# Attention scores of each head in four column tiles of 32 keys, with the queries of a chunk read from one of two fixed buffers

## What is computed

```python
B, N, C = x.shape                      # 4, 4096, 128
q, k, v = jnp.split(jnp.einsum('bnc,ce->bne', x, W_qkv), 3, axis=-1)
...                                    # each to (B, N, 4 heads, 32)
q = l2norm_axis1(q)
k = l2norm_axis1(k)
sim = jnp.einsum('bihd,bjhd->bhij', q, k) * SCALE
attn = jax.nn.softmax(sim, axis=-1)
out = jnp.einsum('bhij,bjhd->bhid', attn, v)
...
return jnp.einsum('bne,ec->bnc', out, W_out) + b_out
```

## Time and profile before

| | |
|---|---|
| median of 3 runs | 6119.24 us (6114.16 to 6120.37) |
| the profiled execution's own time | 6126.93 us |
| its span, first to last instruction | 6125.1 us |
| mean granted TensorE clock | 0.943 of full |
| attention, each of 4 images | about 571 us |
| from one chunk's reciprocal to the next | 70.51 us in most chunks |
| PE / DVE / ACT busy in those 571 us | 552.28 / 518.54 / 495.73 us |

### The profile page before, as it was taken

How to read it: one execution, slowest core, us unless ns; L and a number is a source line. 1 busy time by engine, 2 the same in 40 slices (tenths; PEclk the granted TensorE clock), 3 DMA queues, 4 the chain that set the end, 5 groups by cost and what they waited for, 6 DMA issues and landing times. The chain is left out here.

```text
span 6125.1 us, 76011 instructions
## 1 busy us (share of the span) xinstructions
PE 4839.5 (79%) x21528; PEld 1764.6 (29%) x21592; DVE 5167.2 (84%) x5922; ACT 3730.4 (61%) x4769; POOL 2009.7 (33%) x1562
## 2 busy tenths in 40 slices
PE   5777779996676778999667667899966667789996
PEld 2222422222322242222232224222233222422223
DVE  6799679998679967999868996799976899689987
ACT  1666378882266637888126663788812666378881
POOL 2488500003148850000414884000041588400004
PEclk8899989999889999999888999899988899999998
DMA  1000020000000002000000000200000000020000
GB/s 37 0 1 0 14 53 0 0 0 14 28 0 1 0 14 53 0 0 0 14 28 0 1 0 14 53 0 0 0 19 24 0 1 0 14 53 0 0 0 14
DMA packets 26639, 69.18 MB, mean 11 GB/s; under 512 B 11225, under 2 KB 13089, under 8 KB 23329
## 3 DMA queue, kind: packets, MB, share of 16 engines
q1 hardware_dynamic: 26400, 66.43, 4.3%
HBM read 26.55 MB, written 8.39 MB: 6 GB/s over the span
## 5 line engine op out<-in xcount | busy, mean ns | idle before, releaser
L1257 ACT ACTIVATE arena<-ps 128x1024 f32<-128x1024 f32 x2048 | 1982.9, 1024 | 288.0 <-PE ps L1228 250.0
L1272 DVE TENSOR_TENSOR arena<-arena 128x1024 f32<-128x1024 f32 x1664 | 1914.8, 1222 | 134.2 <-ACT arena L1257 134.2
L916 DVE TENSOR_TENSOR_SCAN arena<-ps,hlast,arena 128x512 f32<-128x512 f32 x1024 | 1269.2, 1284 | 5.2 <-DVE arena L898 3.2
L876 POOL TENSOR_TENSOR arena<-arena 128x1024 f32<-128x1024 f32 x512 | 1207.6, 2359 | 22.1
L1228 PE MATMUL ps<-arena 128*128 (+1 forms) x4096 | 1080.4, 385 | 87.4 <-issue 62.2
L1212 PE MATMUL ps<-arena 128*32 128x512 f32 x8192 | 1081.8, 606 | 38.2 <-DVE arena L1277 35.1
L845 ACT ACTIVATE ps<-arena,amat 128x512 f32<-128x512 f32 x1024 | 692.2, 688 | 506.9 <-DVE arena L916 506.2
L813 PE MATMUL ps<-arena,ident 128*128 128x512 f32 x2048 | 972.7, 598 | 7.7 <-POOL arena L876 7.7
L1558 POOL MEMSET arena<- 128x1024 f32 x4 | 3.8, 957 | 2777.0 <-POOLq L101 2777.0
L1228 PEld LDWEIGHTS ps<-arena 128*128 128x128 f16 x4096 | 316.5, 98 | 1197.0 <-ACT arena L1257 806.6
L898 DVE TENSOR_TENSOR arena<-arena,ps 128x1024 f32<-128x1024 f32 x512 | 620.3, 1212 | 47.6 <-remote 29.9
(11 more groups left out here) (245 smaller groups left out, 4931.0 us busy)
## 6 DMA issues: line engine op xcount, KB each, us to landing
arena<-x SPq DMA_DIRECT2D x32, 512.0 KB, 5.8
arena<-arena SPq DMA_DIRECT2D x64, 256.0 KB, 6.0
arena<-arena SPq DMA_DIRECT2D x64, 224.0 KB, 5.7
arena<-pe SPq DMA_DIRECT2D x256, 32.0 KB, 1.8
out<-arena SPq DMA_DIRECT2D x8, 1024.0 KB, 3.9
expw<-L_ffn_expert_w SPq DMA_DIRECT2D x1, 512.0 KB
wqkv<-L_attn_W_qkv SPq DMA_DIRECT2D x1, 192.0 KB
wx<-in_projT SPq DMA_DIRECT2D x1, 128.0 KB
```

Source lines behind the costliest of these rows:

```text
L876: pool.tensor_tensor(halves(g[s % 4]), halves(hb[s % 4]), cs[s % 4].unsqueeze(1).broadcast_to([128, HD, CH]), ALU.mult).then_inc(hc_s, 1)
L916: dve.tensor_tensor_scan(halves(hb[s % 4])[:, h, :], da(s, h), halves(dbx[s % 2])[:, h, :], k.hlast[:, s, h, :], ALU.mult, ALU.add).then_i ...
L1257: act.activation(probs[p % 8], k.bank(2 * group[p], 2 * CH), ACT.Exp, scale=SCALE / SPLIT ** 2).then_inc(exp_s, 1)
L1272: dve.tensor_tensor(acc[p % 2], acc[p % 2], probs[p % 8], ALU.add).then_inc(acc_s, 1)
```

## The change

Each score matmul of 128 keys becomes four of 32 keys at tile positions (0, 0), (0, 32), (0, 64) and (0, 96), which write the four quarters of the same bank. They read `queries`, a view with fixed addresses: for chunk 0 the first 512 columns of `qs`, for the others one of two buffers of 128x4x512 float16 that SP fills, chunk by chunk, with one DMA each. The buffers lie where the low parts of the queries lay. PE's loop of 7 turns of one chunk becomes one of 3 turns of two chunks, and chunk 7 is written out.

```diff
+def staged_queries(k):
+    return [k.at(QL_AT + i * 2 * CH, 2 * CH).bitcast(F16).rearrange("p (h n) -> p h n", h=HEADS) for i in range(2)]
...
-        def body(c, first):
+        def body(c, queries, first):
...
                     for e in range(2):
                         h = 2 * a + e
-                        last = pe.matmul(k.bank(2 * group[p] + e), ks[:, h, j * 128:(j + 1) * 128],
-                                         qs[:, h, cols_of(c)], start=True, stop=True)
+                        for t in range(4):
+                            last = pe.matmul(k.ps[32 * t:32 * t + 32, (2 * group[p] + e) * CH:(2 * group[p] + e + 1) * CH],
+                                             ks[:, h, j * 128 + 32 * t:j * 128 + 32 * t + 32], queries[:, h, :],
+                                             start=True, stop=True, tile_position=(0, 32 * t))
                     last.then_inc(s_mm, 1)
...
-        body(0, True)
-        pe.wait_ge(k.sem("q_rest"), 4 * HEADS * 16)
-        with pe.Fori(1, NCH) as c:
-            body(c, False)
+        def staged(c, i, n):
+            pe.wait_ge(staged_s[i], n * 16)
+            body(c, q_now[i], False)
+
+        body(0, qs[:, :, 0:CH], True)
+        with pe.Fori(0, NCH // 2 - 1) as cc:
+            staged(cc * 2 + 1, 1, cc + 1)
+            staged(cc * 2 + 2, 0, cc + 1)
+        staged(NCH - 1, 1, NCH // 2)
...
             sp.wait_ge(k.sem("q_rest"), 4 * HEADS * 16)
+            for c in range(1, NCH):
+                if c >= 3:
+                    sp.wait_ge(k.sem("scores_mm"), (c - 1) * 2 * (L // 128))
+                sp.dma_start(staged_queries(k)[c % 2], qs[:, :, cols_of(c)]).then_inc(staged_s[c % 2], 16)
+            for i in range(2):
+                sp.wait_ge(staged_s[i], 16 * ((NCH - 1 + i) // 2))
```

More of the change, by code:

```diff
@@ L1170, in qkv @@
     k.clear()
+def staged_queries(k):
+    return [k.at(QL_AT + i * 2 * CH, 2 * CH).bitcast(F16).rearrange("p (h n) -> p h n", h=HEADS) for i in range(2)]
 def attend(k):
     qs, ks = (k.at(a, 2 * L).bitcast(F16).rearrange("p (h n) -> p h n", h=HEADS) for a in (QS_AT, KS_AT))
+    q_now, staged_s = staged_queries(k), [k.sem("q_even_staged"), k.sem("q_odd_staged")]
     v, ao = k.at(V_AT, L), k.at(TNT_AT, L)
@@ L1431, in _ @@
             sp.wait_ge(k.sem("q_rest"), 4 * HEADS * 16)
+            staged_s = [k.sem("q_even_staged"), k.sem("q_odd_staged")]
+            qs = k.at(QS_AT, 2 * L).bitcast(F16).rearrange("p (h n) -> p h n", h=HEADS)
+            for c in range(1, NCH):
[4 more added lines that the diff above has]
+                sp.wait_ge(staged_s[i], 16 * ((NCH - 1 + i) // 2))
         @block.tensor
```

## The result

The changed kernel takes 6032.11 us (median, 6028.32 to 6033.2), the kernel before 6119.81 in the runs beside it: a ratio of 0.9853, 95% interval 0.9841 to 0.9865, 88 us or 1.5% less. The forecast was 6028, faster.

The account below looks back on a forecast made before the run. PE was taken to bound the attention stages, losing 0.24 us a key tile in tile-shape switches. Steady chunks -126 us and branch misses with half-clock spells +35 gave -91 from 6119.24: 6028 us, range 5985 to 6100.

Parts of the forecast that it names:

- What bounds the kernel before: Attention stages: PE bounds; a key tile takes 1.97 us for 1.72 of streaming, 0.24 lost switching tile shape.
- What is late next: After the change an ordinary key tile falls from 1.97 to 1.85 us; 3.95 us a chunk saved, -126 us.
- the ring: PE's `weigh` and scores and ACT's exponentials wait on each other in turn: 1.85 us an ordinary tile, 2.6 a `direct` one.
- DVE comes close but stays hidden: Over six key tiles, DVE's ten additions need 11.36 us, within the 11.85 us predicted for the stretch.
- two signs that I named: Profile after: DVE's waits for ACT stay, and ACT's waits for PE fall below half.
- Longer loop body: PE's two-chunk loop is taken to miss instruction fetch at all 8 branches back, 4.4 us each; +35 us with half-clock spells.
- half-clock spells: PE idle over 4 us at a branch back risks half clock: 1.65 us each, counted in half of the 8.
- the part of the stall that is hidden: At each branch back 0.6 us of the added 4.2 was taken as hidden, leaving 3.6 exposed.
- the signs I named: Profile after: two chunks per image near 70 to 72 us, PE branch over 4 us, queue 8 busy mid-stage.
- Issue, loads, staging: In PE's stage, more score instructions, their weight loads and SP's 28 query copies were each counted as costing 0.
- the bound on issue: PE instructions start below 10 ns each, from 0.13-0.11 us behind a jump; an ordinary tile allows 39 ns.
- One price of a rival: Rival: score fours, starting g apart, don't stream at full rate; one after another (g = 0.86) adds 2080 us. Chance 0.14.

Follow-up runs that it names:

- e5: Kernel before (128-key scores, one-chunk loop) with each `weigh` placed one key tile later on PE; 6119.28 us against 6122.08, ratio 0.9997.
- e2: Changed kernel with its buffers, DMAs and two-chunk loop, but score matmuls of 128 keys as before; 6139.05 us, ratio 1.003 to the kernel before.
- e4: Changed kernel with each `weigh` placed one key tile later on PE; 5982.46 us, ratio 0.9772 to the kernel before.
- e9: Changed kernel with six key tiles instead of five summed by PE, `weigh` not moved; 6046.36 us, ratio 0.9876 to the kernel before.
- e1: Changed kernel without the query buffers and SP's copies, PE's chunks 1 to 7 written out instead of looped; 6040.06 us.
- e3: Changed kernel, buffers kept, with PE's chunks 1 to 7 written out so no branch back is taken in the stage; 6021.97 us.
- e7: Changed kernel with `weigh` one key tile later (as e4) and six key tiles instead of five summed by PE; 5961.85 us.
- e10: Written-out kernel with later `weigh` and six tiles summed by PE, PE's last sum of a chunk moved ahead of the last `weigh`; 5918.11 us, ratio 0.9669.

## Why the prediction was right, step by step

*What bounds the kernel before: PE, with 0.24 us lost at each key tile in switches of tile shape.* Right. e5 shows the bound (a different order changes nothing, and the 0.24 us are lost all the same), e2 that constant addresses and the buffers give nothing (70.43 us a chunk), and the timelines that a four starts every 0.217 us, that `weigh` to scores lost its 0.12 us, and, once ACT is out of the way (e4), scores to `weigh` too. That the float type costs nothing was read in the scan; after the change, scores follow `weigh` without a gap though the type still changes.

*What is late next: the ring, 1.85 us for an ordinary tile, 11.85 for six, 66.55 a chunk.* 1.84, 11.90 and 66.47 were measured. The 3.95 us a chunk were 4.04: 129 us over 32 chunks, not 126. e4 and e9 show that it is the ring, from both sides. One remark in it was too comfortable: "DVE comes close but stays hidden". DVE is 0.7 us a chunk behind the ring, and works 50 additions on end. I looked at the steady stretch of six tiles, where it has half a microsecond to spare, and not at the chunk as a whole, where it begins some 5 us late. In line with that, two signs that I named were wrong: DVE's waits for ACT didn't stay but fell from 34.6 to 11.8 us, and ACT's for PE fell only from 64.9 to 57.3 (a direct tile's wait is now the ring's).

*Longer loop body: 8 misses, +35 us.* The misses came, all 8, with a branch of 3.35 to 3.87 us where 4.4 was taken. The term was mis-sized. Summed over the 8 chunks, what they take above 66.47 is 3.4+3.7+3.8+3.4+3.3+3.2+1.8+1.6 = 24 us. Two of them hold a dip (1.7 us each) that starts 58 us ahead of their branch, so the branches themselves cost 21 us. The half-clock spells came as counted, in 4 of the 8, right behind the branch; one of them:

```profile
1166.20:1169.60 3.40, 3.40 (x24) 0.94 (x20) 0.00 (x0) 2.59 (x3) 0.00 (x0) 0.50 0.00 0
```

Its branch runs from 1160.89 to 1164.72. What was wrong is the part of the stall that is hidden: I let it be 0.6 us of 4.2 and took 3.6 as exposed; 1.6 to 1.8 us is exposed where no dip comes along. The rows of such a turn show why:

```profile
1026.80 1.94 ACT L1271 ACTIVATE arena<-ps 128x1024 f32<-128x1024 f32 x2 [0.76 <-PE ps L1236]
1026.85 1.04 PE L1219 MATMUL ps<-arena 128*32 128x512 f32 x8
...
1027.94 2.36 DVE L1286 TENSOR_TENSOR arena<-arena 128x1024 f32<-128x1024 f32 x2 [0.34 <-ACT arena L1271]
...
1030.04 1.05 PE L1236 MATMUL ps<-arena 128*32 128x512 f16 x16 [2.15 <-issue]
...
1033.31 3.36 DVE L1288 RECIPROCAL arena<-ps 128x512 f32<-128x512 f32 x1 [3.01 <-PE ps L1208]
```

The branch begins at 1026.3, while PE has queued streams until 1027.89, so PE stands idle 2.15 us of its 3.5. And DVE's last addition ends at 1030.30; it waits 3.01 us for the sum, against 1.32 at a plain turn (963.47 above), which leaves 1.7. Of the signs I named, queue 8 came (294 packets where 98 were); a branch of over 4 us did not, and only 6 of the 8 chunks were near 70, the others at 68.1 and 68.2.

*Issue, loads, staging: nothing.* Right in a steady chunk, wrong in the first one of an image. In a steady chunk loads and streams of a four never show as a wait; e1 and e3 have the same plain chunk. The reasons were thinner than the result. I compared one load of 0.109 us with the 0.216 us of a four, which needs four loads: one after another they would take 0.44 us. They are hidden because they overlap each other, four in 0.12 us:

```profile
939.12 0.12 PEld L1236 LDWEIGHTS ps<-arena 128*32 128x32 f16 x4 [0.30 <-issue]
```

And the 0.11 us that I took off the 0.13 of the earlier trace rows was the load of `weigh`; those of L1228 have a median of 0.098 us, so the bound on issue was nearer 15 ns than 10, still far below 39. The Trainium skill (TensorE: Matmul & The Clock Gate, Part 2, the step on decode) gives some 62 ns for a matmul when the sequencer's program decodes it. This kernel isn't bound by that: eight score matmuls with their loads pass in 0.43 us, 54 ns a matmul, and wait for nothing but ACT.

In chunk 0, behind the jump over the guarded branch, PE's timeline now reads

```profile
824.16 1.90 PE L1236 MATMUL ps<-arena 128*32 128x512 f16 x16 [16.48 <-issue]
829.65 5.31 PE L1236 MATMUL ps<-arena 128*32 128x512 f16 x48 [3.60 <-issue]
```

where 14 streams ran in one piece before (from 828.98, 5.66 us). Sixteen streams, with their loads 32 instructions, and PE stands idle 3.60 us with nothing in the profile to wait for; in the other images it is 2.27, 3.53 and 2.54 us (the profile puts the 2.27 down to ACT). The windows show the clock at half meanwhile, and the DMA engines full of SP's 16 copies of the queries, as before:

```profile
824.00:834.00 10.00, 6.25 (x60) 1.99 (x64) 3.36 (x4) 5.06 (x6) 0.00 (x0) 0.50 1.02 206
```

It is the tiles that bring the gap: e2, which has the buffers and the loop but the wide scores, has none and takes 72.6 us from its first scores to the first reciprocal (the kernel before 72.7), and e1, which has the tiles without the buffers, has gaps of 1.7 to 2.7 us. The same idle time, named issue, is what a branch back leaves, so I read it as a fetch of instructions too, and the packets of queue 8 bear that out: in each image one of 16 KB comes in 1.1 to 2.6 us behind the first scores, and PE goes on 1.5 to 1.7 us after it has ended, 4.2 us behind the first scores where it comes early and 5.5 where it comes late. In the kernel before such a packet comes at about the same time (1.2 to 2.5 us), while the first 14 streams are still running. That four times as many instructions for the same streams use up the first block before the next is there is an inference from these times. From the start of the jump to the first reciprocal the four images now take 78.2, 75.2, 76.3 and 75.1 us, and took 77.9, 77.3, 76.9 and 77.3: 4.5 us gained in all, where four plain chunks gain 16. I priced issue by its rate alone, and not by what has to be fetched behind a jump: a missing term of +12 us.

*The sum.* In profiled spans 93.7 us were gained: 129, less 21 for the branches back with the four dips behind them, less 12 for the first chunks, less 2 for the last chunk of each image (69.93 us before, 66.42 now), and less 2 for the other dips, five before and six after. That makes 92, and the rest is not traced. In medians the gain is 87.7 us. The forecast came within 4 us by luck in part: the branches were put 14 us too high and the steady chunks 3 too low, and against that the first chunks (12), the last ones (2) and the other dips (2) were left out. One price of a rival doesn't come out either: with g = 0.86 a tile is 4.30 us, 2.33 more than 1.97, so +2390 us over 32 chunks of 32 tiles and not +2080; nothing hung on it.

What stays open is when the dip comes. Behind a branch back it starts 0.4 to 1.5 us after the branch has ended, in four cases of eight. Elsewhere it starts 4.1 to 4.8 us behind the start of a reciprocal, where PE has waited for DVE: in nearly all chunks of an image or in none in e1 and e3, in one or two of seven in the kernel before. The runs show no rule for which.

## What to carry to other kernels

Matmuls of different tile shapes in turn cost about 0.12 us at each switch here (e5 against e4); where that happens every microsecond and PE is the bound, the wide matmul split into four column tiles is as fast and takes the switch away, in this kernel 4 us of 70. Before such an edit, work out which ring of waits and which engine are next, over a whole turn of the loop and not over its steady part: here they stood at 66.5 and 65.7 us, and it took a change of order (e4), of share (e7) and of the last sum's place (e10) together to get from 1.5% to 3.3%. And count instructions: a loop of two chunks was too long to stay on the core even with the wide matmuls (e2), and its branches back cost 21 of the 129 us; four times as many matmuls left PE idle behind a jump, which cost some 12 more. Whether a loop of one chunk with tiles, 1632 instructions, would stay was not tried.

## What I had not expected of the hardware

- A loop body of 1728 PE instructions misses at its branch back (3.4 us median, e2), one of 864 does not (0.21 us).
- Dense small matmuls run PE dry behind a jump: idle 2.3 to 3.6 us after the first 16 streams of each attention stage, where wide matmuls ran on (kernel before and e2).
- The half-clock spell can be locked to the loop: 68.24 us from chunk to chunk in one image, 66.54 in the next, in the same run (e3).
- Slack hides stalls better than fewer stalls do: the same 8 branches cost 3.0 us each in the changed kernel, dips counted in, and 0.3 to 1.0 in all but one case with `weigh` one tile later (e4).
